# The last stage's fused activations in two float16 parts, scaled by a power of two, in place of three bfloat16 parts

## The reference, cut to what matters

```python
def _quantized_matmul(x, w, scale):
    wq = w.astype(jnp.float8_e4m3fn).astype(x.dtype)
    y = jnp.einsum('bsi,io->bso', x, wq)
    return y * scale
gate = jax.nn.silu(_quantized_matmul(x, gate_w, gate_scale))   # 256 -> 768
up = _quantized_matmul(x, up_w, up_scale)                      # 256 -> 768
fuse = gate * up
return _quantized_matmul(fuse, down_w, down_scale)             # 768 -> 256
# x = x + tanh(g_ffn[3]) * the above, on _layernorm(x)
```

## Time and profile before

| | us |
|---|---|
| median of 3 runs (lowest, highest) | 986.15 (985.16, 987.31) |
| the profiled execution's own time | 987.38 |
| its span | 985.6 |
| last stage, from the first normalising operation (939.3) to the last VectorE operation (983.1) | 43.8 |

### The profile page before, as it was taken

One profiled execution on the slowest core, in us unless ns is written; L12 is line 12 of the kernel. 1 busy time (PEld: TensorE's weight loads), 2 busy tenths in 40 slices (PEclk: granted clock), 3 DMA queues, 4 the chain that ended last, 5 costly groups with the idle time before them and its releaser, 6 DMA issues. The chain is left out here.

```text
span 985.6 us, 17661 instructions
## 1 busy us (share of the span) xinstructions
PE 903.1 (92%) x5736; PEld 566.4 (57%) x5736; DVE 706.0 (72%) x1411; ACT 609.9 (62%) x1197; POOL 397.3 (40%) x337
## 2 busy tenths in 40 slices
PE   9799989898999999998599988999789999988788
PEld 4555546524777777776377663333556666675436
DVE  6999988889666676666688758997562334258876
ACT  5799945786777777776466475888414433215463
POOL 2899410586455455553232290000014677300132
PEclk9899999999999999999699999999999999989989
DMA  5432067000000000000000490000042232240001
GB/s 152 131 116 98 2 203 224 12 7 10 22 16 16 22 18 21 16 16 1 6 1 1 144 383 26 2 2 3 28 174 66 50 75 44 38 113 0 1 1 43
DMA packets 43976, 56.79 MB, mean 58 GB/s; under 512 B 5712, under 2 KB 34904, under 8 KB 43912
## 3 DMA queue, kind: packets, MB, share of 16 engines
q1 hardware_dynamic: 39880, 50.44, 15.8%
q0 software_dynamic: 4032, 5.51, 3.4%
HBM read 49.64 MB, written 6.23 MB: 57 GB/s over the span
## 5 line engine op out<-in xcount | busy, mean ns | idle before, releaser
L1511 POOL TENSOR_TENSOR a_scratch<-a_scratch,a_inverse 128x512 f32<-128x512 f32 x64 | 66.6, 1041 | 115.1 <-DVE a_inverse L1647 115.1
L2736 PE MATMUL bank<-wup,moe_xT 128*128 x184 | 83.0, 594 | 1.2 <-ACT moe_xT L2803 1.1
L2487 DVE TENSOR_REDUCE a_tops<-bank 128x4 f32<-128x1024 f32 x64 | 77.8, 1224 | 8.4 <-PE bank L2216 5.5
L2382 ACT ACTIVATE a_room<-bank,exp_scale 128x1024 f32<-128x1024 f32 x64 | 71.2, 1114 | 13.7 <-PE bank L2239 13.7
L587 POOL TENSOR_TENSOR ssm_drive<-ssm_du,ssm_b_row 128x1024 f32<-128x1024 f32 x32 | 74.5, 2366 | 3.3 <-DVE ssm_state L664 2.0
L1428 ACT ACTIVATE a_scratch<-bank,a_bias,a_q_factor 128x256 f32<-128x256 f32 x128 | 71.1, 560 | 7.2 <-DVE a_bias L1634 6.8
L664 DVE TENSOR_TENSOR_SCAN ssm_state<-bank,ssm_drive 128x512 f32<-128x512 f32 x64 | 74.6, 1208 | 0.8 <-POOL ssm_drive L587 0.5
L2996 DVE TENSOR_TENSOR moe_act_f<-bank,moe_silu 128x512 f32<-128x512 f32 x23 | 15.9, 692 | 80.7 <-ACT moe_silu L2810 69.0
L1240 PE MATMUL bank<-keys,a_scratch 128*128 (+1 forms) x256 | 69.1, 392 | 1.6 <-DVE xn L1574 0.7
L2803 ACT COPY moe_xT<-bank 128x256 f32<-128x256 f32 x23 | 8.6, 373 | 91.8 <-PE bank L2724 74.4
L424 PE MATMUL bank<-ssm_seen,ident 128*128 128x512 f32 x124 | 63.7, 597 | 1.8 <-ACT ssm_seen L520 1.8
(11 more groups left out here) (528 smaller groups left out, 2361.4 us busy)
## 6 DMA issues: line engine op xcount, KB each, us to landing
ssm_b_row<-ssm_b_spill SPq DMA_DIRECT2D x16, 512.0 KB, 3.6
wup<-in_l_up_dram SPq DMA_DIRECT2D x8, 1024.0 KB, 14.8
a_wq_in<-in_l1x_q_dram SPq DMA_DIRECT2D x32, 128.0 KB, 2.1
wdn<-in_l_down_dram SPq DMA_DIRECT2D x8, 512.0 KB, 9.5
keys<-in_l1x_o_dram SPq DMA_DIRECT2D x1, 2048.0 KB, 13.1
X<-in_x_dram SPq DMA_DIRECT2D x1, 1024.0 KB, 7.9
lora_raw<-in_l_gate_dram SPq DMA_DIRECT2D x1, 1024.0 KB, 5.0
lora_raw<-in_l_up_dram SPq DMA_DIRECT2D x1, 1024.0 KB, 7.1
```

Of the source, the lines that this page charges most:

```text
L1511: pool.tensor_tensor(prob[:, j, :, :], prob[:, j, :, :], inverse[:, j, :].unsqueeze(2).to_broadcast([P, 2, SEQ]), ALU.mult).then_inc(S["p_ ...
L2382: act.activation(prob[:, 2 * (f % 3) + p, :, :], bank[:, at:at + 2, :].rearrange("p j (t n) -> p (j t) n", t=2), ACT.Exp, scale=exp_scale[ ...
L2487: dve.tensor_reduce(tops[:, f // 2 % 3, :, first:first + 2].rearrange("p q h -> p h q"), bank[:, at:at + 2, :].rearrange("p h (q n) -> p h ...
L2736: last = pe.matmul(bank[:, 2 * (i % 2) + m, :], xT[:, i % 2, c, :], wup[:, bass.ds(e, 1), c * 2 * FF + m * FF:c * 2 * FF + (m + 1) * FF] . ...
```

## The change

The three bfloat16 parts of `fuse` become two float16 ones: ScalarE casts (L3424), VectorE subtracts (L3458); GpSimd has no work in the stage and ScalarE's second cast goes. The down weights are held in float16. TensorE does 12 matmuls per output tile.

float16 has a narrow range, so `fuse` is scaled: a bound for the product of gate and up is worked out in the experts' stage from the largest rounded gate weight and gate scale, the largest up weight and up scale. The product of the four is cut to a power of two (its exponent bits alone, `fp_power`). `us` is divided by it (and multiplied with 0.25), `ds` multiplied (and divided by 0.25). What that adds to the experts' stage:

- VectorE: two reductions of 128x1536 over `rounded_w[0]` and `rounded_w[1]` (tiles 6 and 11), two of 128x6 over `gs` and `us` (tile 18), a reduction and a copy of 4x128 ahead of y of tile 18 (in round 20), a copy of 128x4 ahead of y of tile 20 (in round 22), seven chained small operations after the last tile.
- TensorE: a transpose of 128x4 behind `turn_a(19)`, a matmul of 4 columns over 4 rows behind `turn_a(21)`, each behind two waits. They reduce over partitions and spread the result to all.

```diff
-        self.rounded_w = [sb(f"rounded_w{i}", [P, DC * FP_FF], dt) for i, dt in enumerate((F16, F16, BF16))]
+        self.rounded_w = [sb(f"rounded_w{i}", [P, DC * FP_FF], dt) for i, dt in enumerate((F16, F16, F16))]
...
 (stage_moe, TensorE, behind turn_a(i))
+                    if i == 19:
+                        pe.wait_ge(fp_topped, 4)
+                        pe.wait_ge(y_ready, i - 2)
+                        pe.transpose(bank[0:4, 6, DM:DM + P], fp_tops[:, :], core.ident[:, :])
+                    if i == 21:
+                        pe.wait_ge(fp_tops_read, 1)
+                        pe.wait_ge(y_ready, i - 2)
+                        pe.matmul(bank[:, 6, DM:DM + 4], fp_rows[:, :], core.ident[0:4, 0:4], start=True, stop=True)
                     if i >= 1:
                         down(i - 1)
...
 (VectorE, bring_y)
                     dve.wait_ge(down_done, i + 1)
+                    if i == 18:
+                        chain(dve.tensor_reduce(fp_bound[0:4, 0:1], bank[0:4, 6, DM:DM + P], AX.X, ALU.max))
+                        dve.tensor_copy(fp_rows[:, :], fp_bound[0:4, 0:1].to_broadcast([4, P])).then_inc(fp_tops_read, 1)
+                    if i == 20:
+                        dve.wait_ge(fp_tops_read, 1)
+                        chain(dve.tensor_copy(fp_bound[:, :], bank[:, 6, DM:DM + 4]))
...
 (VectorE, round_step)
+                    if w in (1, 2) and k == 0:
+                        dve.wait_ge(rounded, w)
+                        dve.tensor_reduce(fp_tops[:, w - 1:w], core.rounded_w[w - 1][:, :], AX.X, ALU.max, apply_absolute_value=True
+                                          ).then_inc(fp_topped, 1)
...
                         dve.wait_ge(scales_in, 3 * 16)
+                        for n, g in enumerate((core.gs, core.us)):
+                            dve.tensor_reduce(fp_tops[:, 2 + n:3 + n], g[:, :], AX.X, ALU.max, apply_absolute_value=True
+                                              ).then_inc(fp_topped, 1)
+                        dve.wait_ge(fp_topped, 4)
...
                 bring_y(NTILE - 1)
+                chain(dve.tensor_tensor(fp_bound[:, 0:2], fp_bound[:, 0:2], fp_bound[:, 2:4], ALU.mult))
+                chain(dve.tensor_tensor(fp_power[:, :], fp_bound[:, 0:1], fp_bound[:, 1:2], ALU.mult))
+                chain(dve.tensor_scalar(fp_power[:, :], fp_power[:, :], FP_TINY, None, ALU.max))
+                bits = fp_power[:, :].bitcast(mybir.dt.uint32)
+                chain(dve.tensor_scalar(bits, bits, EXPONENT, None, ALU.bitwise_and))
+                chain(dve.reciprocal(fp_factor[:, :], fp_power[:, :]))
+                dve.tensor_scalar(core.us[:, :], core.us[:, :], fp_factor[:, 0:1], FUSED_TOP, ALU.mult, ALU.mult)
+                dve.tensor_scalar(core.ds[:, :], core.ds[:, :], fp_power[:, 0:1], 1.0 / FUSED_TOP, ALU.mult, ALU.mult)
...
 (stage_fp8_ffn)
-        f_rest = s.sb("f_rest", [P, 2, HALF])
-        f_parts = [s.sb(f"f_part{i}", [P, JC, NTOK], BF16) for i in range(3)]
+        f_parts = [s.sb(f"f_part{i}", [P, JC, NTOK], F16) for i in range(2)]
...
-                        for i in range(3):
+                        for i in range(2):
...
-                                             start=j == 0 and i == 0, stop=j == JC - 1 and i == 2)
+                                             start=j == 0 and i == 0, stop=j == JC - 1 and i == 1)
...
-                    if n >= 1:
-                        act.wait_ge(f_rested, n)
-                        act.copy(part_of(1, n - 1), f_rest[:, (n - 1) % 2, :]).then_inc(f_mid, 1)
-                act.wait_ge(f_rested, 2 * JC)
-                act.copy(part_of(1, 2 * JC - 1), f_rest[:, 1, :]).then_inc(f_mid, 1)
-
-            @block.gpsimd
-            def _(pool):
-                for n in range(2 * JC):
-                    pool.wait_ge(f_hi, n + 1)
-                    await_count(pool, f_lo, n - 1)
-                    await_count(pool, f_mid, n - 1)
-                    pool.tensor_tensor(f_rest[:, n % 2, :], fuse[:, n % 2, :], part_of(0, n), ALU.subtract
-                                       ).then_inc(f_rested, 1)
...
-                    dve.wait_ge(f_mid, n + 1)
-                    dve.tensor_tensor(part_of(2, n), f_rest[:, n % 2, :], part_of(1, n), ALU.subtract).then_inc(f_lo, 1)
+                    dve.wait_ge(f_hi, n + 1)
+                    dve.tensor_tensor(part_of(1, n), fuse[:, n % 2, :], part_of(0, n), ALU.subtract).then_inc(f_lo, 1)
...
-                    await_count(dve, f_rested, n - 1)
+                    await_count(dve, f_lo, n - 1)
...
-                    if n >= 2:
-                        low_part(n - 2)
-                low_part(2 * JC - 2)
+                    if n >= 1:
+                        low_part(n - 1)
                 low_part(2 * JC - 1)
```

More of the change, by code:

```diff
@@ L2594, in stage_moe @@
         turn_in = s.sem("turn_in")
+        FUSED_TOP, FP_TINY, EXPONENT = 0.25, 2.0 ** -100, 0x7F800000
+        fp_tops, fp_rows = s.sb("fp_tops", [P, 4]), s.sb("fp_rows", [4, P])
+        fp_bound, fp_power, fp_factor = s.sb("fp_bound", [P, 4]), s.sb("fp_power", [P, 1]), s.sb("fp_factor", [P, 1])
+        fp_topped, fp_tops_read = s.sem("fp_topped"), s.sem("fp_tops_read")
         xn_rows, x_rows = core.xn_rows, core.x_rows
@@ L2623, in twice @@
         def twice(w):
-            return fp_doubled[:, :] if w < 2 else fp_doubled[:, :].bitcast(BF16)
+            return fp_doubled[:, :]
         with nc.Block() as block:
@@ L3352, in stage_fp8_ffn @@
         silu, fuse = s.sb("silu", [P, 2, HALF]), s.sb("fuse", [P, 2, HALF])
-        f_rest = s.sb("f_rest", [P, 2, HALF])
-        f_parts = [s.sb(f"f_part{i}", [P, JC, NTOK], BF16) for i in range(3)]
+        f_parts = [s.sb(f"f_part{i}", [P, JC, NTOK], F16) for i in range(2)]
         scaled = s.sb("scaled", [P, 2, DM])
-        x_hi_ready, x_ready, f_hi, f_rested, f_mid, f_lo = (s.sem(n) for n in (
-            "x_hi_ready", "x_ready", "f_hi", "f_rested", "f_mid", "f_lo"))
+        x_hi_ready, x_ready, f_hi, f_lo = (s.sem(n) for n in ("x_hi_ready", "x_ready", "f_hi", "f_lo"))
         gate_up, silu_done, fused, out_done, times, added, stored = (s.sem(n) for n in (
```

## The result

| | before | changed |
|---|---|---|
| median, us (lowest, highest), 4 runs each | 985.9 (985.16, 987.31) | 979.15 (978.52, 980.02) |
| ratio, 95% interval | | 0.9928 (0.9917 to 0.994) |
| span of the profiled execution | 985.6 | 978.2 |
| experts' stage: mix of its third tile to the next stage's first VectorE operation | 128.29 | 128.51 |
| next stage: from there to the last stage's first VectorE operation | 64.58 | 64.36 |

The account below looks back on a forecast made before the run. TensorE was taken as the bound, 92% busy, with its down projection uncovered and VectorE's splitting stalling gate/up. -5.24 - 1.28 + 0.25 = -6.27 us gave 979.9 from the median 986.15, range 978.8 to 982.6.

Parts of the forecast that it names:

- 48 matmuls, 5.24: Down projection: 48 of 144 TensorE matmuls go, at 0.1092 us each, uncovered, saving 5.24 us.
- The stall, 1.28: Gate/up part: VectorE's low part falls to 0.69 us with GpSimd idle, so TensorE's 1.28 us of stall go.
- rival A: Gate/up part: the low part stays near 1.23 us for its types, stall kept, 981.2 us; chance 0.12.
- The tail, slack 1.5: Last stage's end: low part covered before the fifth tile, VectorE 1.5 us ahead at the last output tile, cost 0.
- The experts' stage, 0.25: Experts' stage: the added transpose and small matmul cost full TensorE 0.25 us; VectorE's additions and the waits cost 0.
- The sum, -6.27: Whole kernel: matmul and stall savings less the experts' stage's additions, -6.27 us, 979.9 from the median.
- Rival B: Gate/up or experts' rounds: VectorE loses its step or additions delay rounds, 3 to 4 us come back, 983.4; chance 0.11.
- C: Last stage: TensorE's clock stays at 1.2 GHz for the first half of gate/up, 990.3 us; chance 0.03.
- D: Down projection: its time is what feeds the matmuls, so 48 fewer give nothing, 986 us; chance 0.04.

Follow-up runs that it names:

- experiment 3: Changed kernel with the low part's matmul issued twice, so 18 matmuls per output tile again; 985.33 us, ratio 0.9986 to the kernel before.
- experiment 4: Kernel before the change with only two of its three parts summed, all three still made; 983.6 us, ratio 0.997 to the unedited one.
- experiment 1: Changed kernel plus, in each of 12 blocks, a GpSimd subtraction of two SBUF inputs that nobody waits for; 982.12 us, ratio 0.9961.
- experiment 2: Changed kernel plus, in each of 12 blocks, a GpSimd iota that writes SBUF and reads nothing; 980.18 us, ratio 0.9944.
- experiment 5: Changed kernel with the low part's subtraction on GpSimd in place of VectorE; 979.7 us, ratio 0.9937.
- experiment 8: Changed kernel with 4 matmuls without use in TensorE's idle gap before the last stage; 979.07 us in one run.
- experiment 7: Changed kernel with 11 matmuls without use in TensorE's idle gap before the last stage; 980.45 us, ratio 0.9942.
- experiment 9: Changed kernel with 11 matmuls without use before the last stage and its first block's matmuls reordered, high part first; 978.29 us, ratio 0.9919.

## Why the prediction was right

- *48 matmuls, 5.24.* It is 5.24 in the chain (15.73 - 10.49). As a price of matmuls it is right by experiment 3 (5.26). As a gain of that edit alone it would have been wrong: 3.69 (experiment 4). The tail's part of the sum, which found the fifth tile covered with the low part at 968.0, used the new chain already; experiment 4 shows its remark that an uncovered low part costs what it is late.
- *The stall, 1.28.* 20.37 to 19.13 is 1.24. That GpSimd's reads lengthen a VectorE operation with two inputs in SBUF is shown by experiments 1, 2 and 5, and rival A (types) is out: 0.68 us with float16 output. That VectorE's length was the stall is read from the trace of before; how near ScalarE's three operations stood to the same limit (experiment 1) the prediction didn't weigh, and since the second cast went too, it made no difference. VectorE's block was put at 1.44, with nothing for the fuse's new wait for the low part; the wait's 0.14 us in experiment 1 would leave it under 1.735 all the same.
- *The tail, slack 1.5.* It was 1.4.
- *The experts' stage, 0.25.* It was 0.22 there, with bounds of 0.2 to 0.55. The waits held nothing up.
- *Not foreseen:* the next stage gave the 0.22 back, so the net was near 0.
- *The sum, -6.27* from the median 986.15, is 979.9 against 979.15. The last stage's two terms were 6.52 and it gave 6.51. The other 0.24 of the 6.75 are within what unchanged code scatters, so that the whole came out 0.75 under the forecast says nothing for or against a term.
- Rival B had the loop lose its step: it closed at 1.735 with VectorE 0.4 us idle a block, and the rounds with the reductions kept their 5.82. C: the clock was back at 1.00 before the second block, as before the change, and stayed there. D is out by experiment 3.

The rule of the Trainium skill that the prediction weighed ("SBUF — State Buffer", "Who interferes with whom") agrees with experiments 1 and 2, its distinction between GpSimd's reads (low part 1.26 us) and writes (0.68) included. The traces add that the exclusion is a little short of the whole instruction: the low part ended 0.54 to 0.55 us after GpSimd, with 0.68 of its own to do.

## What to carry to other kernels

When an operation has two durations in one trace, look for what ran beside the long ones before putting the price down to its shape: here a VectorE subtraction cost 0.68 us, or 1.24 on the mean while GpSimd was reading, and the choice of engine for a neighbour was worth a block's stall. Two edits on one path need not add: fewer matmuls uncover the latency of what feeds them, so work out the tail with both in place. Price what is added to a full engine from rows of that stage, and look at the stage behind before calling the time lost.

## What the runs showed of the hardware beyond the forecast

- The gap after which TensorE's clock falls is not one number: it fell 0.9 us after the last product in the changed kernel (at 933.3), held through 4.8 us of idle with 4 matmuls ahead of it (experiment 8), and fell 1.0 us into busy transposes behind a gap of 1.75 in one profile of two (experiments 7 and 9).
- A VectorE subtraction that starts 0.12 us behind GpSimd's ends 0.55 us after it, one that starts 0.88 behind ends 0.54 after it (experiment 1, at 951.12), and so does the one of the earlier trace rows, 0.44 behind. So most of GpSimd's remaining duration is waited for, not shared, and the low part lasts longer the earlier it meets it: 1.70 us or 0.93.
- VectorE's additions to `X`, with two tensors in SBUF, took 0.77 and 0.93 us beside GpSimd's subtractions and 0.48 without them; beside the same subtractions its multiplications with one tensor in PSUM kept their 0.41 and 0.75 (experiment 5).
